# Two ones-products of the attention, moved up behind the third group of value products

## The chip, the cores and the metric

The kernel runs on one core of one Trainium2 chip. The metric is the device time of one launch in microseconds (us), as the median of several runs.

## The reference

Cut to what the change touches, the reference is a cross attention. Its queries come from `x` (2 batches, 1024 rows, width 256), its keys and values from a context of 77 rows joined to `x`, so there are 1101 keys. It has 16 heads of width 64:

```
q, k, v = split_heads(...)                       # 16 heads, 64 wide
dots = einsum('bhid,bhjd->bhij', q, k) * scale
attn = softmax(dots, axis=-1)
out  = einsum('bhij,bhjd->bhid', attn, v)
x    = x + out.reshape(...) @ Wout
```

Behind it stands a mixture of 32 experts with routing, which the change does not touch.

## The kernel before, in words

**Tiling.** Heads are worked in pairs: 8 pairs, one `turn` each. Within a pair the 2048 queries are cut into four blocks of 512 (`d` = 0 to 3; batch is `d // 2`), so the attention is 32 blocks. A block has 18 score tiles: head `h` = 0, 1 of the pair by key tile `kt` = 0 to 8 (the last has 77 keys). An event ("st", d, h, kt) is one such tile: TensorE makes scores with two products (L817, L821), ScalarE takes the exponential into `probsT` (L1458), and the event ("add", d, h, kt) adds the tile to a running row sum on GpSimd (L636).

**The other events of a block.**
- "av" (L832): two value products per key tile, accumulated in `ps_o`. Tiles 0 to 2 come at (1, 3) of the block's own walk, 3 to 5 at (1, 6), and tiles 6 to 8, the third group, only in the walk of the next block, behind its score tile (0, 5). ScalarE then copies `ps_o` to `oT` (L1446).
- "max" (L794 on TensorE, L1246 on VectorE): scores of 128 queries against all keys, reduced to the negated row maximum. The four of head 1 of a block come at (0, 0) to (0, 5) of the same block; `own_max[3]` is the last.
- "row" (L800, L1253): when the four maxima of a head are there, TensorE turns them into a row (it waits for `max_done`), and VectorE writes them into `q2`. The second score product (L821) of the head's first tile waits for that.
- "sum" (L844, L1257): two products of `rowsum` with ones give the sums over the keys for both heads. TensorE waits for the last add of that block. VectorE takes the reciprocal of the result into `rinv`.
- "norm" (L641, GpSimd): `oT` times `rinv`. "out" (L857, L1267): the product with `Wout`, added to `x_sb`.
- "k", "q", "v" (L720) project keys, queries and values for a coming block; "hi" (ScalarE, L1430, L1432) and "lo" (VectorE, L1235, L1238) split them into a high and a low part. `q_again` and `q_low`, the last parts of the query split, stand at (0, 5) in every block.

**What sets the order.** `attention_plan()` writes one list of events out by hand, and every engine walks the same list in order and does its own part of each event. Where an event stands in the list sets its place in the queue of TensorE, VectorE, ScalarE and GpSimd at once. Events in `IN_RING`, "sum" among them, take the two PSUM banks `ps_t` in turn, by their order in the list (`job_in`); an event waits until the one two places before it has released its bank.

The plan of a block is in `after`, a map from a score tile to what follows it. `prev` is the block before. In block 0 of the first pair there is no block before it, and "sum" is a placeholder that only passes its bank on; the sum of the very last block stands in the list END, behind the walk.

Of the kernel before, what the change touches and what calls it, by code (L numbers as in the profile page):

```python
# [60 lines left out]
def attention_plan():  # L61

    turn = []
    for d in range(QUADS):
        n, ahead = (d + 1) % QUADS, -int(d == LAST_D)
        prev, behind = (d - 1) % QUADS, int(d == 0)
        b = n // 2  # L70
        project = n % 2 == 0

        def nxt(*ev):
            return ev, ahead

        def own(*ev):
            return ev, 0

        def old(*ev):
            return ev, behind  # L80

        def values(make, block, kts):
            return [make("av", block, kt) for kt in kts]

        def project_q():
            return [nxt("q", b, n % 2), nxt("hi", "q", b, n % 2, (0, 1))]

        def project_k(i):
            return [nxt("k", b, i), nxt("hi", "k", b, i, (0, 1))]

        q_again, q_low = nxt("hi", "q", b, n % 2, (2, 3)), nxt("lo", "q", b, n % 2)
        k_low = [nxt("lo", "k", b, i) for i in range(3)]
        first_values = values(own, d, (0, 1, 2))
        more_values = values(own, d, (3, 4, 5))
        last_values = values(old, prev, (6, 7, 8))
        own_max = [own("max", d, 1, i) for i in range(4)]
        next_max = [nxt("max", n, 0, i) for i in range(4)]
        out = [old("out", prev, i) for i in range(2)]
        after = {(0, 8): [own("row", d, 1), old("sum", prev)],
                 (1, 1): [],  # L100
                 (1, 2): [old("norm", prev), next_max[0]],
                 (1, 3): first_values + [next_max[1]]}
        if project:
            after[0, 0] = [own_max[0]] + project_k(0) + [own_max[1], k_low[0]]
            after[0, 2] = project_k(2) + [own_max[2], k_low[2]]
            after[0, 3] = project_k(1) + [k_low[1]]
            after[0, 5] = project_q() + [q_again] + last_values + [q_low, own_max[3]]
            after[1, 4] = [out[0], next_max[2]]
            after[1, 5] = [nxt("v", b, 0), next_max[3]]
            after[1, 6] = more_values + [nxt("row", n, 0), out[1]]  # L110
            after[1, 7] = [nxt("v", b, 1)]
            after[1, 8] = [nxt("v", b, 2)]
        else:
            after[0, 0] = [own_max[0]] + project_q() + [own_max[1]]
            after[0, 3] = [own_max[2]]
            after[0, 5] = [q_again] + last_values + [q_low, own_max[3]]
            after[1, 4] = [out[0], next_max[2]]
            after[1, 6] = [out[1], next_max[3]] + more_values + [nxt("row", n, 0)]
        if d == 2:
            after[1, 1] = [(("w", 0), -1)]  # L120
        for h in range(2):
            for kt in range(KEY_TILES):
                turn += [own("st", d, h, kt)] + ([own("add", d, h, kt)] if kt else []) + after.get((h, kt), [])

    before = [("w", 0)]
    for i in (0, 2, 1):
        before += [("k", 0, i), ("hi", "k", 0, i, (0, 1)), ("lo", "k", 0, i)]
    before += [("q", 0, 0), ("hi", "q", 0, 0, (0, 1)), ("hi", "q", 0, 0, (2, 3)), ("v", 0, 0), ("max", 0, 0, 0),
               ("lo", "q", 0, 0), ("v", 0, 1), ("max", 0, 0, 1), ("v", 0, 2), ("max", 0, 0, 2), ("max", 0, 0, 3),
               ("row", 0, 0)]  # L130
    before = [(ev, -1) for ev in before]
    assert sorted(map(str, before)) == sorted(str(item) for item in turn if item[1] == -1)

    def stand_in(ev, back):
        if ev[0] == "out" and back == 1:
            return [(("cen", ev[2]), 0)]
        return [(("gap", ev), 0)] if ev[0] in IN_RING else []

    def stand_in_router(events):

        put = {("st", 2, 1, 8): [("stat", 0)],
               ("st", 3, 0, 1): [("root", 0), ("normed", 0), ("normed", 1)],
               ("st", 3, 0, 2): [("turned", 0, 0)],
               ("st", 3, 0, 3): [("low", 0, 0)],
               ("st", 3, 0, 4): [("low", 0, 1)],
               ("st", 3, 0, 5): [("low", 1, 0)],
               ("st", 3, 0, 6): [("square", 0), ("low", 1, 1)],
               ("st", 3, 0, 8): [("square", 1)]}
        done = []
        for ev, back in events:  # L150
            done += [(new, 0) for new in put.get(ev, [])]
            turned = ev[0] == "gap" and d_of(done) == LAST_D and JOB_OF_TURN.get(ev[1])
            if turned != ("turned", 0, 0):
                done.append((turned, 0) if turned else (ev, back))
        return done

    def d_of(events):
        return max((ev[1] for ev, back in events if ev[0] == "st"), default=0)

    first = [item for ev, back in turn for item in ([(ev, back)] if back < 1 else stand_in(ev, back))]  # L160
    final = [item for ev, back in turn for item in ([(ev, back)] if back >= 0 else stand_in(ev, back))]
    final = stand_in_router(final)
    end = [item for item in turn if item[1] == 1] + [(("gap", ("pad",)), 1)]
    at = [ev[0] for ev, back in end]
    end.insert(at.index("sum") + 1, (("stat", 2), 1))
    end.insert(at.index("sum") + 2, (("score", 0), 1))
    return before, first, turn, final, end


def xattn_moe(nc, x, ctx_in, ln_m_g, ln_m_b, ln_l_g, ln_l_b, Wq, Wkv, Wout, group_c, expert_c, e_bias,  # L170
# [28 lines left out]

    JOBS_A = B * DT * 2 + DT  # L200
    BEFORE, FIRST, TURN, FINAL, END = attention_plan()
    SCORES = [ev for ev, back in TURN if ev[0] == "st"]
    RING, BEFORE_RING, END_RING = ([ev[1] if ev[0] == "gap" else ev for ev, back in events
# [1403 lines left out]
```

## Time and profile before

| | |
|---|---|
| median of 3 runs | 1681.18 us (1678.7 to 1681.22) |
| span of the profiled execution, first to last instruction | 1731.2 us |
| TensorE busy in it | 1541.0 us, 89% |
| VectorE, ScalarE, GpSimd busy | 58%, 46%, 54% |
| attention blocks, from the first row product to the last block's reciprocal | 69.5 to 1122.7 us |
| mean granted TensorE clock | 0.950 of 2.4 GHz |

The page names no device time of the profiled execution other than its span. The span is 50.0 us longer than the median of the runs. In timelines each line is a run of like instructions on one engine: start, time until its end, engine, line and operation, number of instructions, and in brackets how long the engine sat idle before it and what released it. Matmul ends are modelled and reach past the start of the next matmul, so distances between starts are the better measure for TensorE. One product in full f32 shows as two MATMUL instructions.

### The profile page before, as it was taken

How to read it: one execution, taken by the hardware profiler on the slowest of the kernel's cores; microseconds unless marked ns; L12 is line 12 of the kernel's file. 1: busy time of each engine (PE TensorE's matmuls, PEld its weight loads, DVE VectorE, ACT ScalarE, POOL GpSimd, SP SyncE). 2: the span in 40 equal slices, each digit the busy share in tenths (PEclk: the TensorE clock that was granted, in tenths of full speed). 3: DMA queues.
4: the chain of work that ended last, by engine and by line, in shares of the span. 5: the costliest groups of instructions: out<-in, count | busy, mean ns of one | idle time of the engine just before them, and what ended most of it. 6: DMA issues, size and time to landing. Idle time of an engine off the chain costs nothing.

```text
span 1731.2 us, 25990 instructions
## 1 busy us (share of the span) xinstructions
PE 1541.0 (89%) x8078; PEld 1075.6 (62%) x8078; DVE 999.6 (58%) x1517; ACT 800.9 (46%) x1548; POOL 939.7 (54%) x748
## 2 busy tenths in 40 slices
PE   2799999999999999999999998853488999999995
PEld 1555555555555555555555555442477999999995
DVE  5455565565565565565565565483135666666663
ACT  2344544544544544544544544431125666666663
POOL 3366676676676676676676676535701334343433
PEclk8799999999999999999999999856798999999998
DMA  9600000000000000000000000022305667676664
GB/s 228 138 14 10 14 14 10 14 13 9 13 13 9 13 13 9 13 13 9 13 13 9 14 13 1 1 93 84 116 24 169 182 176 187 166 192 171 183 173 92
DMA packets 92700, 114.28 MB, mean 66 GB/s; under 512 B 10195, under 2 KB 71637, under 8 KB 92629
## 3 DMA queue, kind: packets, MB, share of 16 engines
q1 hardware_dynamic: 75605, 93.82, 18.8%
q0 software_dynamic: 17056, 19.97, 5.9%
q8 instruction: 20, 0.33, 0.1%
q14 instruction: 19, 0.16, 0.0%
HBM read 71.78 MB, written 35.06 MB: 62 GB/s over the span
## 4 chain that ended last, share of the span: by engine, by line
PE 80%; DVE 7%; ACT 5%; issue 3%; another core or an unknown queue 3%; DMA 1%; POOL 0%; SPq 0%; DVEq 0%; ACTq 0%; POOLq 0%
PE ps_o L832 15%; PE ps_t L720 9%; PE ps_m L794 9%; PE ps_st L817 8%; PE ps_m L720 8%; PE ps_st L720 7%; PE ps_st L821 6%; ACT arena L1458 3%; PE ps_t L857 3%; PE ps_o L913 3%; PE ps_m L913 3%; PE ps_t L844 2%; PE ps_t L939 2%; PE ps_t L800 1%
## 5 line engine op out<-in xcount | busy, mean ns | idle before, releaser
L636 POOL TENSOR_TENSOR arena<-arena 128x512 f32<-128x512 f32 (+1 forms) x512 | 656.3, 1284 | 370.9 <-ACT arena L1458 346.8
L1458 ACT ACTIVATE arena<-ps_st 128x512 f32<-128x512 f32 (+1 forms) x576 | 326.3, 595 | 434.9 <-PE ps_st L821 420.9
L1246 DVE TENSOR_REDUCE arena_r<-ps_m 128x1 fp32r<-128x1101 f32 x256 | 332.3, 1298 | 234.4 <-PE ps_m L794 230.7
L678 POOL DMA_INDIRECT acc_rows<-arena,ids x96 | 151.8, 1581 | 315.7 <-ACT arena L1555 288.2
L817 PE MATMUL ps_st<-arena_r 128*128 128x512 f32 (+1 forms) x576 | 262.6, 456 | 24.2 <-ACT arena L1458 24.2
L832 PE MATMUL ps_o<-arena 128*64 128x512 f32 (+1 forms) x1152 | 268.4, 601 | 0.0
L821 PE MATMUL ps_st<-arena_r 68*128 68x512 f32 (+2 forms) x576 | 229.6, 399 | 0.9 <-DVE arena_r L1253 0.9
L794 PE MATMUL ps_m<-arena_r 128*128 128x512 f32 (+1 forms) x768 | 193.0, 360 | 6.3 <-DVE arena_r L1246 6.3
L794 PEld LDWEIGHTS ps_m<-arena_r 128*128 128x128 f32 x768 | 134.6, 192 | 102.7 <-issue 44.6
L817 PEld LDWEIGHTS ps_st<-arena_r 128*128 128x128 f32 (+1 forms) x576 | 106.9, 186 | 111.9 <-ACT arena L1458 87.9
L1507 ACT ACTIVATE arena<-ps_m 128x320 f32<-128x320 f32 (+1 forms) x144 | 65.7, 456 | 234.6 <-PE ps_st L720 166.8
L720 PE MATMUL ps_m<-arena_r 128*128 128x320 f32 (+2 forms) x864 | 164.8, 327 | 2.1 <-DVE arena_r L1337 1.3
L832 PEld LDWEIGHTS ps_o<-arena 128*64 128x64 f32 (+1 forms) x1152 | 74.3, 136 | 141.3 <-issue 130.5
L1295 DVE TENSOR_TENSOR arena<-arena,ps_st 128x320 f32<-128x320 f32 (+1 forms) x144 | 73.2, 509 | 152.1 <-ACT arena L1507 126.2
L720 PE MATMUL ps_st<-arena_r 128*128 128x320 f32 (+2 forms) x864 | 159.1, 320 | 0.0
L1280 DVE TENSOR_TENSOR arena_r<-arena,arena_r 128x768 fp32r<-128x768 f32 x128 | 122.1, 956 | 45.4 <-ACT arena_r L1495 40.9
L720 PEld LDWEIGHTS ps_m<-arena_r 128*128 128x128 f32 x864 | 137.0, 191 | 12.0 <-issue 6.8
L720 PEld LDWEIGHTS ps_st<-arena_r 128*128 128x128 f32 x864 | 137.0, 189 | 4.3
L720 PE MATMUL ps_t<-arena_r 128*128 128x512 f32 x384 | 107.7, 418 | 10.4 <-DVE arena_r L1225 6.8
L1257 DVE RECIPROCAL arena<-ps_t 128x512 f32<-128x512 f32 x32 | 107.4, 3358 | 15.9 <-PE ps_t L844 15.9
L821 PEld LDWEIGHTS ps_st<-arena_r 68*128 68x128 f32 (+2 forms) x576 | 107.9, 187 | 11.3 <-DVE arena_r L1253 2.0
L1495 ACT ACTIVATE arena_r<-arena 128x768 fp32r<-128x768 f32 x132 | 110.3, 841 | 5.2 <-PE ps_t L913 5.2
(175 smaller groups left out, 1802.7 us busy)
## 6 DMA issues: line engine op xcount, KB each, us to landing
arena<-in_L_ffn_wg_dram SPq DMA_DIRECT2D x32, 512.0 KB
arena<-in_L_ffn_wu_dram SPq DMA_DIRECT2D x32, 512.0 KB
arena<-in_L_ffn_wd_dram SPq DMA_DIRECT2D x32, 512.0 KB
x_slots<-arena SPq DMA_DIRECT2D x5, 2176.0 KB, 19.9
arena<-x_slots SPq DMA_DIRECT2D x32, 272.0 KB, 2.7
arena_r<-arena_r SPq DMA_DIRECT2D x30, 275.2 KB, 3.6
arena<-x_slots SPq DMA_DIRECT2D x32, 68.0 KB, 2.4
x_sb<-in_x_dram SPq DMA_DIRECT2D x2, 1024.0 KB, 7.4
```

The source lines that it names most:

```text
L636: pool.tensor_tensor(acc, probsT[0:rows, h, 0, :] if kt == 1 else acc, probsT[0:rows, h, kt, :], ALU.add).then_inc(added, 1)
L678: pool.indirect_dma_start(out=dst[:, :], in_=y_sb[par][:, c, 0:w], in_offset=None, compute_op=ALU.add, out_offset=bass.IndirectOffsetOnAxi ...
L720: mm = pe.matmul(ps, a, m, start=(n == 0), stop=(n == len(pairs) - 1))
L794: mm = pe.matmul(scores_m[:, lo:lo + w], q1[h][:, c:c + P], k1[b][h][:, lo:lo + w], start=True, stop=True)
L817: pe.matmul(ps_st[0:rows, n % 2, :], k1[b][h][:, r], q1[h][:, c:c + 512], start=True, stop=False)
L821: pe.matmul(ps_st[0:rows, n % 2, :], k2[b][h][kr, r], q2[h][kr, c:c + 512], start=False, stop=True).then_inc(st_ready, 1)
L832: mm = pe.matmul(ps_o[ROWK[h], :], vals[0:rows, d // 2, kt, ROWK[h]], probsT[0:rows, h, kt, :], start=(kt == 0), stop=(kt == KT_N - 1), sk ...
L1246: dve.tensor_reduce(neg[h][:, c:c + 1], scores_m[:, 0:KEYS], AX.X, ALU.max, negate=True)\
L1257: dve.reciprocal(rinv[:, :], bank[:, :]).then_inc(free, 1)
L1280: dve.tensor_tensor(ws_lo[slot][:, c], w_raw[slot][:, c], ws_hi[slot][:, c].bitcast(F32), ALU.subtract).then_inc(w_lo_done, 1)
L1458: act.activation(probsT[0:rows, h, kt, :], ps_st[0:rows, n % 2, :], ACT.Exp)\
L1495: act.activation(ws_hi[slot][:, c], w_raw[slot][:, c], ACT.Copy).then_inc(w_hi_done, 1)
```

## The change

"sum" of the previous block leaves the place behind score tile (0, 8), where it stood behind "row", and goes to the end of `last_values`, which stands at (0, 5) in front of `q_low` and `own_max[3]`.

```diff
         more_values = values(own, d, (3, 4, 5))
-        last_values = values(old, prev, (6, 7, 8))
+        last_values = values(old, prev, (6, 7, 8)) + [old("sum", prev)]
         own_max = [own("max", d, 1, i) for i in range(4)]
...
-        after = {(0, 8): [own("row", d, 1), old("sum", prev)],
+        after = {(0, 8): [own("row", d, 1)],
                  (1, 1): [],
```

The two uses of `last_values`, unchanged by the diff:

```
after[0, 5] = project_q() + [q_again] + last_values + [q_low, own_max[3]]   # d = 1, 3
after[0, 5] = [q_again] + last_values + [q_low, own_max[3]]                 # d = 0, 2
```

## Rows read from the trace of the kernel before

**Rows 1.** The page: span, busy time of TensorE, engine shares of the chain

```profile
span 1731.2 us, 25990 instructions
...
PE 1541.0 (89%) x8078; PEld 1075.6 (62%) x8078; DVE 999.6 (58%) x1517; ACT 800.9 (46%) x1548; POOL 939.7 (54%) x748
...
PE 80%; DVE 7%; ACT 5%; issue 3%; another core or an unknown queue 3%; DMA 1%; POOL 0%; SPq 0%; DVEq 0%; ACTq 0%; POOLq 0%
```

**Rows 2.** Busy time by stretch, attention: start:end, length, busy per engine, clock, DMA

```profile
89.70:1076.00 986.30, 962.59 (x4307) 567.89 (x4306) 590.62 (x555) 460.16 (x837) 658.17 (x516) 1.00 0.05 12
```

**Rows 3.** The waits of TensorE's matmuls: us in total, times, longest

```profile
PE ps_st L817 <- ACT arena L1458: 24.2, 95, 1.6
...
PE ps_m L794 <- DVE arena_r L1246: 6.3, 6, 3.1
...
PE ps_st L821 <- DVE arena_r L1253: 0.9, 2, 0.5
```

**Rows 4.** Timeline of TensorE, a block with d = 1

```profile
504.65 0.78 PE L794 MATMUL ps_m<-arena_r 128*128 128x512 f32 x3
...
507.24 0.49 PE L800 MATMUL ps_t<-ident,arena_r 128*128 128x512 f32 x1
507.67 1.08 PE L844 MATMUL ps_t<-arena,ones 128*64 128x512 f32 x4
508.68 0.51 PE L817 MATMUL ps_st<-arena_r 128*128 128x512 f32 x1
...
511.81 2.79 PE L832 MATMUL ps_o<-arena 128*64 128x512 f32 x12
```

**Rows 5.** Timeline of VectorE: the reciprocal of the block before, then the same block

```profile
476.36 3.36 DVE L1257 RECIPROCAL arena<-ps_t 128x512 f32<-128x512 f32 x1 [0.34 <-PE ps_t L844]
...
504.46 1.39 DVE L1238 SCALAR_TENSOR_TENSOR arena_r<-ps_t,arena_r 64x512 fp32r<-64x512 f32 x2 [2.16 <-ACT arena_r L1432]
505.88 1.30 DVE L1246 TENSOR_REDUCE arena_r<-ps_m 128x1 fp32r<-128x1101 f32 x1
...
508.79 3.36 DVE L1257 RECIPROCAL arena<-ps_t 128x512 f32<-128x512 f32 x1 [0.34 <-PE ps_t L844]
512.07 1.24 DVE L1246 TENSOR_REDUCE arena_r<-ps_m 128x1 fp32r<-128x1101 f32 x1
```

**Rows 6.** The instructions of L1257: shortest, median, longest ns, first and last start

```profile
L1257 DVE RECIPROCAL arena<-ps_t x32: 3357/3358/3358, 119.1 to 1119.3; 128x512 f32<-128x512 f32 x32
```

**Rows 7.** Timeline of TensorE, the block with d = 2 that follows

```profile
537.29 0.77 PE L794 MATMUL ps_m<-arena_r 128*128 128x512 f32 x3
...
539.82 0.39 PE L800 MATMUL ps_t<-ident,arena_r 128*128 128x512 f32 x1
540.14 1.08 PE L844 MATMUL ps_t<-arena,ones 128*64 128x512 f32 x4
```

**Rows 8.** Timeline of GpSimd: last add of the block before that one

```profile
528.38 1.30 POOL L636 TENSOR_TENSOR arena<-arena 77x512 f32<-77x512 f32 x1 [0.99 <-ACT arena L1458]
```

**Rows 9.** Timeline of TensorE, the very first block, which has no sum

```profile
84.44 0.47 PE L800 MATMUL ps_t<-ident,arena_r 128*128 128x512 f32 x1 [1.54 <-DVE arena_r L1246]
...
85.69 0.79 PE L821 MATMUL ps_st<-arena_r 128*128 128x512 f32 x1 [0.54 <-DVE arena_r L1253]
...
89.74 2.80 PE L832 MATMUL ps_o<-arena 128*64 128x512 f32 x12
```

**Rows 10.** Busy time by stretch, around that first block's row; the clock is third from the end

```profile
85.00:86.00 1.00, 0.46 (x2) 0.31 (x2) 0.63 (x1) 0.00 (x0) 0.89 (x1) 0.84 0.00 0
...
88.00:89.00 1.00, 1.00 (x3) 0.75 (x3) 0.00 (x0) 0.57 (x1) 1.00 (x1) 0.50 0.00 0
89.00:90.00 1.00, 1.00 (x6) 0.53 (x6) 0.69 (x1) 0.17 (x2) 1.00 (x2) 0.95 0.00 0
```

**Rows 11.** The same view earlier, a longer low stretch: its first and last slice of 1 us

```profile
69.00:70.00 1.00, 0.46 (x1) 0.49 (x2) 0.39 (x1) 0.00 (x0) 0.00 (x0) 0.50 0.94 200
...
75.00:76.00 1.00, 1.00 (x6) 0.81 (x5) 0.00 (x0) 0.46 (x1) 0.00 (x0) 0.78 0.00 0
```

## The prediction

> **What bounds the kernel now.** I read the page first: TensorE is busy most of the span and carries 80% of the chain that ended last [rows 1]. An average hides stages, so I then took the stretch of the attention: from 89.70 to 1076.00 TensorE is busy for 962.6 of 986.3 us at a granted clock of 1.00, that is 2.4 GHz [rows 2]. Only 23.7 us of it are idle. Then the list of waits: in the whole span TensorE's matmuls of the attention wait 24.2 us for exponentials, 6.3 us for a maximum and 0.9 us for a row [rows 3]. So nearly nothing is left to win here by shifting work, and whatever makes TensorE wait is paid in full. Last I read one block's timeline on TensorE beside the same on VectorE, because VectorE must do something between any two steps that the change swaps [rows 4, 5, 7].
>
> **What is moved.** Each engine walks one list, so the move is made in every queue. On TensorE the two ones-products (four instructions, 508.68 - 507.67 = 1.01 us from start to start [rows 4]) go ahead of `own_max[3]`, three score tiles and "row". No product is added, so their work costs nothing by itself. On VectorE the reciprocal goes ahead of `q_low`, the reduction of `own_max[3]` and "row". It is 3.36 us long in all 32 cases [rows 6]. ScalarE, GpSimd and SP issue nothing for "sum". "norm" on GpSimd keeps its place at (1, 2) and finds `rinv` ready earlier, which wins at most a part of the 23.7 us of rows 2, since "out" on TensorE is what waits for it. No DMA moves.
>
> **Can the sum run that early?** It waits for the last add of the block before, which ends at 528.38 + 1.30 = 529.68 [rows 8]; the sum would start at 537.29, where the third value products are through [rows 7]. That is 7.6 us of slack, so this wait costs nothing. The banks: "sum" and "row" change places in the ring. "sum" then takes the bank of the last `k` or `v` product before it, released well before; "row" takes that of `q`, released by `q_low`, which VectorE does anyway before the maximum that "row" waits for. Nothing is added.
>
> **Where the path breaks.** "row" on TensorE waits for `max_done` of `own_max[3]`. Now that reduction is short of work ahead of it: `q_low` starts at 504.46, the reduction at 505.88, and it ends at 507.18; "row" starts at 507.24, just as the last score tile is through [rows 4, 5]. So the wait is already on the edge, and any delay on VectorE there shows on TensorE. From the start of the sum in its new place:
> - VectorE: 1.12 us until the reciprocal starts (508.79 - 507.67), 3.28 until the next instruction (512.07 - 508.79), 1.42 for the two halves of `q_low` (505.88 - 504.46), 1.30 for the reduction, 0.06 until "row" starts [rows 4, 5]. Sum 7.18 us.
> - TensorE: 1.01 for the sum, then `own_max[3]` and three score tiles, 507.24 - 504.65 = 2.59 us in blocks with d = 1, 3 [rows 4] and 539.82 - 537.29 = 2.53 us in the others [rows 7]. Sum 3.60 and 3.54 us.
>
> TensorE waits for the difference, 3.58 and 3.64 us, mean **3.61 us a block**. Behind the waiting "row" stand the first score tile of head 1 and so all of ScalarE's exponentials and GpSimd's adds. They can't help.
>
> **What follows the row.** Until now the sum stood between "row" and the first score tile and gave VectorE 1.01 us in which to write `q2`. That cover is gone: the second score product waits for it. The trace has this case: in the very first block "sum" is only a placeholder. There "row" came 1.54 us late, the second score product then waited 0.54 us, and from "row" to the first value product it took 89.74 - 84.44 = 5.30 us [rows 9]. In a normal block it is 511.81 - 507.24 = 4.57 us, less 1.01 for the sum, 3.56 [rows 4]. The difference is **1.74 us**: 0.54 of wait, and 1.20 because the granted clock fell to 0.50 (1.2 GHz). It fell in the slice from 85 to 86, whose mean is 0.84, and was back early in the slice from 89 to 90, whose mean is 0.95 [rows 10]. If TensorE loses the clock after a wait of 1.54 us, I expect it after one of 3.61 us. For the cost of that I have bounds: nothing, if the clock stays, and 3.2 us, if it stays low as long as in the longer low stretch (below). I take 1.20, since that row is nearest in place and in what follows.
>
> The Trainium skill, TensorE: Matmul & The Clock Gate, section Terms, gives the penalty as throttled time times (1 - K/N), half the throttled time here. In the first block that would be half of about 3.4 us (85.68 to 89.10 from the two slice means), 1.7 us in place of 1.20; the trace gives less, since TensorE was waiting for part of it. By the page's figure the sum below would be 31 x 5.86 = 182 us and the time 1863 us.
>
> **The sum.** 3.61 + 0.54 + 1.20 = 5.35 us a block. The move counts in 31 of the 32 blocks: the first has no sum, and the sum of the last stands in the end list, which the change leaves in its order. 31 x 5.35 = 165.9 us. The profiled execution would have a span of 1731.2 + 165.9 = 1897 us. The page gives no other time for it, and its span is 50.0 us (3%) above the median of the runs; I add the same microseconds to the median: 1681.2 + 165.9 = **1847 us**. If everything in the timed runs is 3% shorter, it is 161 us and 1842.
>
> **Rivals.**
> - *The clock stays at 2.4 GHz.* Then only the waits count: 31 x 4.15 = 129 us, **1810 us**. For it: the blocks are otherwise dense, with 0.24 us idle per 10 us [rows 2]. Against it: the first block [rows 9, 10]. Chance 0.20.
> - *The clock stays low for longer.* Near 70 us it was low from before 69.00 to about 75.44 (slice mean 0.78), some 6.4 us [rows 11]. Half of that is 3.2 us a block: 31 x (3.61 + 0.54 + 3.2) = 228 us, **1909 us**. Against it: TensorE was waiting several times in that stretch, which a block here does once. Chance 0.13.
> - *Something takes up most of the wait*, so that a block loses less than 3.8 us and the time stays under 1800 us: for instance the exponential waits of 24.2 us [rows 3] go away, and TensorE reaches "row" later for another cause. What TensorE waits for now is too little for that. Chance 0.03.
> - *The other side: the reciprocal was in the way where it stood.* Now the next maximum is reduced at 512.07, the moment the reciprocal is through [rows 5]. Freed of it, VectorE could run ahead for the next block, and TensorE would lose its present waits, at most the 23.7 us idle of rows 2: **1657 us**. It decides only if VectorE gets from the new sum to the end of the maximum in about 3.6 us; it needs 7.18, of which the reciprocal alone is 3.28. And TensorE shows nearly no wait for a maximum to win [rows 3]. Chance 0.03 (0.02 faster, 0.01 no change).
> - That the change does nothing is excluded by the list: it is one list for all engines, and both places are reached in 31 blocks.
>
> **The numbers.** The forecast has 0.61. Its own range is 1823 (all present idle time of rows 2 gone) to 1863. The range for 8 in 10 takes in the clock that stays and part of the way to the longer low stretch: 1800 to 1895 us. Some 0.2%, 3.4 us, is what a measurement of this kernel can tell from no change. Faster 0.02, same 0.01, slower 0.97.
>
> **What would show it.** In the changed profile: the reciprocal starts 1.1 us after the sum, right behind the third value products; `q_low` starts at its end with no idle time of its own; "row" (L800) has some 3.6 us of idle time before it, released by the maximum (L1246), in 31 blocks, near 112 us in total; L821 waits for L1253 in each block, near 17 us in total; the mean granted clock of the attention falls below 1.00, with a low stretch in each block. The distance between two reciprocals grows from 508.79 - 476.36 = 32.4 us [rows 5] to near 37.8. The expert stage is as before. I am wrong if "row" has no wait, if VectorE does `q_low` before the reciprocal, or if the clock stays at 1.00, which would give the first rival.

## The result, and the profile after

The changed kernel takes **1866.11 us** (median of 4 runs, 1858.18 to 1866.26) against 1680.62 us before (4 runs, 1678.7 to 1681.22). The ratio is 1.109, interval 1.107 to 1.111: 185.5 us slower, 6.0 us for each of the 31 blocks that the move reaches. The forecast was 1847 us, range 1800 to 1895.

One caution on the spans. That of the profile before (1731.2 us) has a disturbance of some 50 us behind the attention: from the end of its last reciprocal to the end it takes 608.5 us, in the changed kernel 1856.4 - 1302.8 = 553.6 us. So differences are taken between run times, or within the attention.

The page of the changed kernel, to be read against [rows 1]:

```profile
span 1856.4 us, 25990 instructions
...
PE 1601.1 (86%) x8078; PEld 1107.4 (60%) x8078; DVE 1005.5 (54%) x1517; ACT 804.2 (43%) x1548; POOL 938.4 (51%) x748
...
PE 76%; DVE 13%; issue 6%; ACT 3%; DMA 1%; POOL 0%; DVEq 0%; SPq 0%; ACTq 0%; POOLq 0%
```

The number of instructions is the same. VectorE's share of the chain (the work that ended last, followed back from the end) went from 7% to 13%, though VectorE is busy for only 6 us more than before. TensorE is busy for 60 us more with the same products, which fits its lower granted clock: 0.91 on average from 113 to 1250 us, against 1.00 in the attention before [rows 2]. The list of waits of TensorE's matmuls names the first cause, to be read against [rows 3]:

```profile
PE ps_t L800 <- DVE arena_r L1246: 108.3, 32, 3.6
...
PE ps_st L817 <- ACT arena L1458: 16.0, 64, 0.8
PE ps_st L821 <- DVE arena_r L1253: 13.2, 33, 0.5
```

"row" (L800) waits 3.6 us at the longest for the maximum; before it was 3.0 us in all. The wait of L821 for VectorE's write of the row is new as well, 0.9 us before. Waits for exponentials fell by 8 us. The place where they went is the one behind the row: at 510.10 TensorE waited 0.22 us for an exponential, and at 585.75 in the changed kernel, where it runs at the lower clock, it doesn't wait. That ScalarE catches up during the long wait is not the reason: with the same pause and the clock at full speed (E9 below) the list has 23.5 us again.

The timeline of TensorE in a block with d = 1, against [rows 4]:

```profile
572.83 2.80 PE L832 MATMUL ps_o<-arena 128*64 128x512 f32 x12
575.46 1.03 PE L844 MATMUL ps_t<-arena,ones 128*64 128x512 f32 x4
576.42 0.78 PE L794 MATMUL ps_m<-arena_r 128*128 128x512 f32 x3
...
582.71 0.80 PE L800 MATMUL ps_t<-ident,arena_r 128*128 128x512 f32 x1 [3.60 <-DVE arena_r L1246]
583.30 0.63 PE L817 MATMUL ps_st<-arena_r 128*128 128x512 f32 x1
584.27 0.80 PE L821 MATMUL ps_st<-arena_r 128*128 128x512 f32 x1 [0.35 <-DVE arena_r L1253]
...
585.75 0.80 PE L817 MATMUL ps_st<-arena_r 128*128 128x512 f32 x1
...
588.82 2.79 PE L832 MATMUL ps_o<-arena 128*64 128x512 f32 x12
```

And VectorE beside it, against [rows 5]:

```profile
576.54 3.36 DVE L1257 RECIPROCAL arena<-ps_t 128x512 f32<-128x512 f32 x1 [3.33 <-PE ps_t L844]
579.93 1.39 DVE L1238 SCALAR_TENSOR_TENSOR arena_r<-ps_t,arena_r 64x512 fp32r<-64x512 f32 x2
581.35 1.30 DVE L1246 TENSOR_REDUCE arena_r<-ps_m 128x1 fp32r<-128x1101 f32 x1
583.54 0.68 DVE L1253 TENSOR_TENSOR arena_r<-ps_t,mask 4x512 fp32r<-4x512 f32 x1 [0.89 <-PE ps_t L800]
```

VectorE goes from the reciprocal to `q_low` to the maximum without idle time: 582.71 - 575.46 = 7.25 us from the sum to "row", of which TensorE can fill 3.6. Before the reciprocal it stood idle for 3.33 us. In the kernel before, `q_low` started 504.46 - 501.92 = 2.54 us after the value products; counted from 572.83 that is 575.37, 1.2 us ahead of the reciprocal, so most of `q_low` would have fitted in front of it. The start of the value products in the kernel before, in front of [rows 4]:

```profile
501.92 2.80 PE L832 MATMUL ps_o<-arena 128*64 128x512 f32 x12
```

The clock by slices of 1 us around the same row (third figure from the end), against [rows 10]:

```profile
544.00:545.00 1.00, 0.46 (x3) 0.12 (x1) 0.68 (x1) 0.00 (x0) 0.00 (x0) 0.69 0.00 0
551.00:552.00 1.00, 1.00 (x6) 0.29 (x4) 0.00 (x0) 0.00 (x0) 1.00 (x2) 0.90 0.00 0
581.00:582.00 1.00, 0.00 (x0) 0.00 (x0) 0.97 (x2) 0.00 (x0) 0.92 (x2) 0.96 0.00 0
582.00:583.00 1.00, 0.29 (x1) 0.29 (x2) 0.65 (x1) 0.00 (x0) 0.47 (x1) 0.50 0.00 0
588.00:589.00 1.00, 1.00 (x4) 0.35 (x5) 1.00 (x1) 0.07 (x1) 1.00 (x1) 0.62 0.00 0
589.00:590.00 1.00, 1.00 (x6) 0.30 (x6) 0.24 (x1) 0.52 (x1) 1.00 (x2) 1.00 0.00 0
```

The granted clock falls to 0.50 (1.2 GHz) at 581.9, while TensorE still waits, and is back at 588.8 (0.62 is 0.24 us at full clock): 6.8 us low. In the block before, whose row starts at 543.62, it fell at 544.4 (0.69 in that slice) and was back at 551.2: 6.8 us as well. The same view over the whole attention has a low stretch at each of the 30 rows that waited 3.4 us or more: 6.8 us long at 24 of them, 10.2 at four, 3.4 at two. In the very first block of the kernel before it had been 3.4 us. From row to value products it takes 588.82 - 582.71 = 6.11 us, where the first block took 5.30.

### The profile page after: what moved, and what is told of

Same layout as the page of the kernel before. It is cut to its first block, busy times and chain, and to the rows that moved or that the text cites. A ratio compares the mean times of both kernels' runs of the same rounds, so it can differ in the third digit from the quotient of the medians.

```text
span 1856.4 us, 25990 instructions
## 1 busy us (share of the span) xinstructions
PE 1601.1 (86%) x8078; PEld 1107.4 (60%) x8078; DVE 1005.5 (54%) x1517; ACT 804.2 (43%) x1548; POOL 938.4 (51%) x748
## 3 DMA queue, kind: packets, MB, share of 16 engines
q1 hardware_dynamic: 75605, 93.82, 17.5%
## 4 chain that ended last, share of the span: by engine, by line
PE 76%; DVE 13%; issue 6%; ACT 3%; DMA 1%; POOL 0%; DVEq 0%; SPq 0%; ACTq 0%; POOLq 0%
PE ps_o L832 14%; PE ps_t L720 9%; PE ps_m L720 8%; PE ps_m L794 8%; PE ps_st L720 7%; PE ps_st L817 7%; PE ps_st L821 7%; DVE arena_r L1246 3%; PE ps_t L857 3%; PE ps_o L913 2%; PE ps_m L913 2%; DVE arena_r L1238 2%; PE ps_t L800 2%; PE ps_t L939 2%; PE ps_t L844 2%
## 5 line engine op out<-in xcount | busy, mean ns | idle before, releaser
L636 POOL TENSOR_TENSOR arena<-arena 128x512 f32<-128x512 f32 (+1 forms) x512 | 655.0, 1279 | 553.6 <-ACT arena L1458 530.1
L817 PE MATMUL ps_st<-arena_r 128*128 128x512 f32 (+1 forms) x576 | 286.3, 497 | 16.0 <-ACT arena L1458 16.0
L832 PE MATMUL ps_o<-arena 128*64 128x512 f32 (+1 forms) x1152 | 276.2, 615 | 0.0
L821 PE MATMUL ps_st<-arena_r 68*128 68x512 f32 (+2 forms) x576 | 260.3, 452 | 13.2 <-DVE arena_r L1253 13.2
L794 PEld LDWEIGHTS ps_m<-arena_r 128*128 128x128 f32 x768 | 146.8, 208 | 107.3 <-issue 50.3
L794 PE MATMUL ps_m<-arena_r 128*128 128x512 f32 (+1 forms) x768 | 204.7, 378 | 6.3 <-DVE arena_r L1246 6.2
L817 PEld LDWEIGHTS ps_st<-arena_r 128*128 128x128 f32 (+1 forms) x576 | 120.6, 209 | 81.7 <-ACT arena L1458 59.6
L1257 DVE RECIPROCAL arena<-ps_t 128x512 f32<-128x512 f32 x32 | 107.4, 3358 | 107.1 <-PE ps_t L844 107.1
L821 PEld LDWEIGHTS ps_st<-arena_r 68*128 68x128 f32 (+2 forms) x576 | 122.2, 212 | 45.1 <-DVE arena_r L1253 34.3
L720 PEld LDWEIGHTS ps_m<-arena_r 128*128 128x128 f32 x864 | 136.1, 190 | 10.8 <-issue 6.7
L800 PE MATMUL ps_t<-ident,arena_r 128*128 128x512 f32 x64 | 38.8, 607 | 110.3 <-DVE arena_r L1246 108.3
```

Of the source, the lines that this page charges most:

```text
L636: pool.tensor_tensor(acc, probsT[0:rows, h, 0, :] if kt == 1 else acc, probsT[0:rows, h, kt, :], ALU.add).then_inc(added, 1)
L720: mm = pe.matmul(ps, a, m, start=(n == 0), stop=(n == len(pairs) - 1))
L794: mm = pe.matmul(scores_m[:, lo:lo + w], q1[h][:, c:c + P], k1[b][h][:, lo:lo + w], start=True, stop=True)
L800: pe.matmul(bank[:, :], neg[h], ident4[:, :, :].rearrange("p a n -> p (a n)"), start=True, stop=True).then_inc(job_ready[jn % 2], 1)
L817: pe.matmul(ps_st[0:rows, n % 2, :], k1[b][h][:, r], q1[h][:, c:c + 512], start=True, stop=False)
L821: pe.matmul(ps_st[0:rows, n % 2, :], k2[b][h][kr, r], q2[h][kr, c:c + 512], start=False, stop=True).then_inc(st_ready, 1)
```

## The experiments

The theory: VectorE's one queue now has the reciprocal ahead of the last maximum and of `q_low`; TensorE waits for that, and the waits cost it the clock. The rival: the cost lies on TensorE's side, in the order of its products or in the changed turn of the two `ps_t` banks. Two further questions: how much is the clock, and was the reciprocal in the way at its old place?

**E1, the reciprocal alone at its old place.** The ones-products stay at (0, 5) as in the changed kernel; VectorE takes the reciprocal at a new event behind "row".

```diff
-        after = {(0, 8): [own("row", d, 1)],
+        after = {(0, 8): [own("row", d, 1), old("recip", prev)],
...
-                    if kind == "sum":
+                    if kind == "recip":
+                        jn, more = own_job(("sum", a), turn)
+                        bank, free = ps_t[jn % 2], job_free[jn % 2]
```

> The products with ones stand at their new place, VectorE's reciprocal at its old one. My theory (the reciprocal queued ahead of the last maximum makes TensorE wait at the row): L800 has no wait for the maximum worth naming; only the cover behind the row is gone, so L821 waits about 0.5 us a block for L1253, 31 x 0.5 = 17 us, and the time is about 1697 us; somewhat more if those short waits cost TensorE's clock. Rival (the cost lies in TensorE's own order or in the changed turn of the two ps_t banks): near the changed kernel, 1866 us.

Measured: **1692.02 us**, ratio 1.007 (1.005 to 1.009). Its waits:

```profile
PE ps_st L817 <- ACT arena L1460: 24.0, 95, 0.9
...
PE ps_st L821 <- DVE arena_r L1253: 17.5, 33, 0.5
...
PE ps_m L794 <- DVE arena_r L1246: 6.7, 6, 3.1
```

The wait of "row" for a maximum stands further down with 3.0 us in all, as before; the 17.5 us of L821 are the lost cover. So TensorE's order and the banks, both as in the changed kernel, cost 11 us of the 185. The rival falls. It is 5 us cheaper than expected. A part of that can be read from starts: behind the value products, TensorE goes on to the sum after 575.46 - 572.83 = 2.63 us, where it took 504.65 - 501.92 = 2.73 to go on to `own_max[3]` before, and the sum itself takes 576.42 - 575.46 = 0.96 in place of 1.01 [rows 4]. E1 has the same 2.63 and 0.96. That is 0.15 us a block, 4.7 us in all.

**E2, `q_low` ahead of the sum.**

```diff
-            after[0, 5] = [q_again] + last_values + [q_low, own_max[3]]
+            after[0, 5] = [q_again] + last_values + [q_low] + ones_sum + [own_max[3]]
```

(The same in the line for d = 1, 3, with `last_values` without the sum and `ones_sum = [old("sum", prev)]`.)

> As the changed kernel, but q_low stands ahead of the sum, so the reciprocal no longer delays it. My theory: the path on VectorE from the sum to the row is 7.18 - 1.42 = 5.76 us, against 3.57 on TensorE, so L800 waits 2.2 us a block (about 68 us in all, 108.3 in the changed kernel), L821 0.4 us as there. If the clock falls as in the changed kernel (about 2.3 us a block), the time is 1680.6 + 31 x 4.9 = 1833 us; if it costs only the 1.2 us that the first block shows, 1799 us. Rival (TensorE's order or the banks): 1866 us, since they are unchanged.

Measured: **1834.22 us**, ratio 1.092 (1.090 to 1.093).

```profile
PE ps_t L801 <- DVE arena_r L1247: 66.9, 32, 2.3
...
PE ps_st L818 <- ACT arena L1459: 15.9, 64, 0.8
...
PE ps_st L822 <- DVE arena_r L1254: 12.3, 33, 0.5
```

The wait of the row (one line lower here) is 66.9 us for an expected 68, longest 2.3. Taking 1.4 us of other work out of VectorE's path takes 1.3 us off each wait. The price of the clock stayed: the waits shrank by 41 us, the time by only 32, and the low stretches at the rows are 6.8 us long as in the changed kernel.

**E3, idle products in the wait, in the row's bank.** Ahead of the row's wait for the maximum:

```diff
+                        for _ in range(14 * h):
+                            pe.matmul(bank[:, :], ident4[:, 0, :], ident4[:, :, :].rearrange("p a n -> p (a n)"),
+                                      start=True, stop=True)
                         pe.wait_ge(max_done, hp * MAX_HP + d * 8 + h * 4 + 4 + 1)
```

> The changed kernel with 14 idle products (identity by identity, into the row's own bank, overwritten by the row) ahead of each wait of a head-1 row, some 0.235 us each, 3.3 us a block, so that TensorE works where it waited. My theory (what the changed kernel loses beyond its waits is the granted clock): clock of the attention back at 1.00, the waits themselves stay as filled or idle time, 31 x (3.6 + 0.5) = 127 us, time about 1808 us. Rival (the rest is lost elsewhere, not in the clock): 1866 us or above. If 14 products outlast the wait, a few us more.

Measured: **1895.08 us**, ratio 1.129 (1.127 to 1.131). The experiment was badly built: the row's bank is now that of `q`, released by `q_low`, so the fill itself had to wait and came behind it, as the timeline of TensorE shows:

```profile
592.26 5.07 PE L800 MATMUL ps_t<-ident 128*128 128x512 f32 x14 [2.26 <-DVE arena_r L1241]
597.17 0.39 PE L803 MATMUL ps_t<-ident,arena_r 128*128 128x512 f32 x1
```

The fill made the block longer instead of filling the wait. The mean clock over the span rose to 0.954, but since the fill came on top of a wait, its cost can't be parted from the clock's. The run does show the bank wait that I had passed over as harmless: harmless for "row", not for anything put before it. The 5.07 us of the 14 products also mislead, because a low stretch of 3.4 us lies over them. A block earlier the same 14 ran at full clock, in 557.14 - 553.81 = 3.33 us, 0.24 each:

```profile
553.81 3.49 PE L800 MATMUL ps_t<-ident 128*128 128x512 f32 x14 [2.08 <-DVE arena_r L1241]
557.14 0.40 PE L803 MATMUL ps_t<-ident,arena_r 128*128 128x512 f32 x1
```

The clock in the two fills (third figure from the end):

```profile
555.00:556.00 1.00, 1.00 (x7) 0.79 (x5) 0.09 (x1) 0.00 (x0) 0.12 (x1) 1.00 0.00 0
...
594.00:595.00 1.00, 1.00 (x4) 0.71 (x4) 0.00 (x0) 0.00 (x0) 0.00 (x0) 0.50 0.00 0
```

**E4, a copy in place of the reciprocal**, in the changed kernel. It leaves out the division by the sums:

```diff
-                        dve.reciprocal(rinv[:, :], bank[:, :]).then_inc(free, 1)
+                        dve.tensor_copy(rinv[:, :], bank[:, :]).then_inc(free, 1)
```

> The changed kernel with a plain copy in place of the reciprocal, so the division by the sums is left out (rinv holds the sums). About 0.69 us in place of 3.36. My theory: the path on VectorE is 7.18 - 2.67 = 4.5 us against 3.57, so L800 waits some 0.9 us a block and L821 0.5: 31 x 1.4 = 45 us, time about 1725 us if the clock holds, up to 1760 if it falls in part of the blocks. Rival (TensorE's order or the banks): 1866 us, since only the length of one VectorE instruction changes.

Measured: **1760.8 us** (1746.53 to 1783.42), ratio 1.044 (1.039 to 1.049) without the longest run. The copy takes 0.69 us, and the row's wait is down to 29.2 us, of which 3.0 stood there before: 0.85 us a block.

```profile
PE ps_t L800 <- DVE arena_r L1246: 29.2, 32, 1.5
```

With TensorE's program untouched, the length of one VectorE instruction decides 105 us. The clock is lost in part of the blocks even with so short a wait: 21 of 30 rows of the attention have a low stretch at them, 9 have none. The runs spread over 37 us where other kernels' spread over 8.1 or less, and their order is that of their mean clock: 1746.5 us at 0.948, 1760.7 and 1761.0 at 0.937, 1783.4 at 0.924. That is one and the same kernel, paying more or less for the clock.

**E5, 9 idle products that wait for nothing late.** Behind score tile (0, 8), into the `ps_st` bank that the next score tile overwrites:

```diff
+                    if kind == "row" and ev[2] == 1:
+                        at = SCORES.index(("st", a, 1, 0))
+                        pe.wait_ge(exp_done, hp * ST_HP + at + 1)
+                        for _ in range(9):
+                            pe.matmul(ps_st[:, at % 2, :], ident4[:, 0, :], ident4[:, :, :].rearrange("p a n -> p (a n)"),
+                                      start=True, stop=True)
```

> The changed kernel with 9 idle products (identity by identity) behind score tile (0, 8), now into the bank of ps_st that the next score tile overwrites, so that they need not wait for the row's bank, which q_low releases. The earlier fill took 5.07 us for 14 products, 0.36 each, so 9 are 3.2 us of the 3.6 us wait. If what the changed kernel loses beyond its waits is the granted clock: clock of the attention near 1.00, L800 waits some 0.4 us a block, time 1680.8 + 31 x (3.5 + 0.4) = 1802 us, 60 us below the changed kernel though TensorE has more to do. Rival (the rest is not the clock): 1866 us or more.

Measured: **1836.12 us**, ratio 1.093 (1.092 to 1.095), 30 us below the changed kernel. The products were shorter than reckoned, 0.25 us each, since the 0.36 came from the fill of E3 at the lower clock. So 1.3 us of wait were left in the block shown:

```profile
607.04 2.27 PE L761 MATMUL ps_st<-ident 128*128 128x512 f32 x9
610.61 0.50 PE L806 MATMUL ps_t<-ident,arena_r 128*128 128x512 f32 x1 [1.29 <-DVE arena_r L1252]
```

Half of the expected gain. The direction was right, the amount open, so the fill was made longer.

**E9, the same with 14.**

> As the fill of 9 products, with 14. In that run the 9 took 2.27 us from start to start, 1.3 us of wait were left ahead of the row, and the mean clock of the attention rose from 0.91 to 0.96. 14 products are 3.5 us and leave next to no wait. If the loss beyond the waits is the clock: clock near 1.00 in the attention, time 1680 + 31 x (3.6 + 0.5) = 1807 us, below the fill of 9 (1836 us) with more work done. Rival (the loss has another cause): as the fill of 9 or above, 1836 us or more.

Measured: **1806.07 us**, ratio 1.075 (1.073 to 1.077), for an expected 1807. The fill covers the wait:

```profile
630.05 3.42 PE L761 MATMUL ps_st<-ident 128*128 128x512 f32 x14
633.80 0.50 PE L806 MATMUL ps_t<-ident,arena_r 128*128 128x512 f32 x1 [0.33 <-DVE arena_r L1252]
```

And the clock of the attention is back, in the busy time by stretch:

```profile
120.00:1050.00 930.00, 891.15 (x3969) 541.46 (x3969) 500.74 (x462) 385.10 (x700) 554.74 (x433) 1.00 0.04 10
```

TensorE does 14 more products a block and the kernel is 60 us faster than the changed one. This takes the loss apart: **126 us are waits** (1806 - 1680), 4.06 us a block, and **60 us are the clock** (1866 - 1806), 1.9 us a block. The 60 us are a net figure: the changed kernel has 12 us less of the short waits than E9 (L817 16.0 against 23.5 us, L821 13.2 against 17.6), which its slower TensorE hides.

The mean clock over the whole span says the same, in order the changed kernel and E9:

```profile
core 0: 1856.4 us, clock 0.915
```

```profile
core 0: 1803.9 us, clock 0.970
```

At two levels, the share at the lower one is twice what is missing to 1: 2 x 0.085 x 1856 = 316 us and 2 x 0.030 x 1804 = 108 us. So 208 us more at 1.2 GHz cost 1858.2 - 1805.7 = 52 us in these two executions, a quarter and not the half. Part of the reason can be read in the block shown: of the 6.8 us, TensorE was idle for 0.8 ahead of "row" (582.71 - 581.92) and 0.35 behind it, and the wait for an exponential that it has at full clock was not there.

**E6, the sum behind `own_max[3]`.**

```diff
-            after[0, 5] = [q_again] + last_values + [q_low, own_max[3]]
+            after[0, 5] = [q_again] + last_values + [q_low, own_max[3]] + ones_sum
```

> The sum at (0, 5), but behind own_max[3]. My theory (an order on VectorE): the maximum is no longer late, so L800 has no wait; but the reciprocal now stands ahead of VectorE's part of the row: it starts near 507.2 in the times of the kernel before, ends at 510.5, the row is written by 511.2 and L821, due at 508.9, waits 2.3 us a block for L1253, 31 x 2.35 = 73 us in all. With a clock loss of 1.4 to 2.8 us a block as in the copy and q_low runs: 1797 to 1840 us. Rival (only the delay of the maximum matters): about 1692 us, as with the late reciprocal.

Measured: **1794.45 us**, ratio 1.069 (1.067 to 1.072), just below the expected span of 1797 to 1840. The wait moved to where the theory put it:

```profile
PE ps_st L822 <- DVE arena_r L1254: 63.0, 33, 2.3
```

VectorE has the reciprocal ahead of the row's write: it starts at 551.22 and the write follows at 554.60 without idle time.

```profile
551.22 3.35 DVE L1258 RECIPROCAL arena<-ps_t 128x512 f32<-128x512 f32 x1
554.60 0.68 DVE L1254 TENSOR_TENSOR arena_r<-ps_t,mask 4x512 fp32r<-4x512 f32 x1
```

So the delay of the maximum isn't the point by itself. The two short urgent steps of VectorE, the maximum and the row's write, both pay when the reciprocal is ahead of them.

**E7, the same copy in the kernel before**, without the division here too.

> The kernel before with a copy in place of the reciprocal: the division by the sums is left out. If the reciprocal at its old place is fully hidden (my theory), only the last one, behind the last block, is on the path: 2.7 us less, 1678 us. Rival (the other side: the reciprocal was in the way where it stood): TensorE's waits in the attention shrink, 1657 to 1670 us.

Measured: **1678.28 us**, ratio 0.999 (0.998 to 1.000), expected 1678. An instruction that is 2.67 us shorter in every block gains 1.7 us in all. At its old place it was hidden.

**E8, the two ones-products taken apart**, head 0 behind tile (0, 7), as a new event `half`, and head 1 at the old place, in the kernel before:

```diff
+                 (0, 7): half_sum,
...
-                        for h in range(2):
-                            mm = pe.matmul(bank[ROWK[h], :], ones[:, 0:DH], rowsum[:, a % 2, h, :],
-                                           start=True, stop=True, skip_group_check=True)
+                        mm = pe.matmul(bank[ROWK[1], :], ones[:, 0:DH], rowsum[:, a % 2, 1, :],
+                                       start=True, stop=True, skip_group_check=True)
```

> The kernel before with its two products with ones taken apart: head 0 behind score tile (0, 7), head 1 where both stood, behind the row. If the waits for exponentials ahead of tile (0, 8), some 0.22 us a block, can be covered with 0.5 us of other work while 0.5 us behind the row still covers VectorE's write: 31 x 0.22 = 7 us less, 1674 us. Rival (the wait only moves to the next tile, or VectorE's write shows): 1681 us or a few more.

Measured: **1697.42 us**, ratio 1.010 (1.009 to 1.012), a miss. The waits for exponentials fell as expected, from 24.2 to 15.8 us. But one product alone costs as much as the pair did: 514.36 - 513.36 = 1.00 us, against 1.01 for both [rows 4]. With 0.38 us won by each wait that is gone (start to start, see E10), 31 x (1.00 - 0.38) = 19 us more were due; 17 are measured.

```profile
513.36 1.07 PE L852 MATMUL ps_t<-arena,ones 128*64 128x512 f32 x2
514.36 0.45 PE L819 MATMUL ps_st<-arena_r 128*77 128x512 f32 x1
```

**E10 and E11, moves into small waits** of the kernel before. E10 puts `next_max[0]` one tile earlier; E11 also moves the next block's "row" from (1, 6) to (1, 7) for d = 0, 2.

```diff
-                 (1, 1): [],
-                 (1, 2): [old("norm", prev), next_max[0]],
+                 (1, 1): [next_max[0]],
+                 (1, 2): [old("norm", prev)],
...
-            after[1, 1] = [(("w", 0), -1)]
+            after[1, 1] = [(("w", 0), -1), next_max[0]]
```

> The kernel before with next_max[0] moved from behind tile (1, 2) to behind tile (1, 1). Its products, 0.5 us on TensorE, then stand where TensorE waits 0.22 us for an exponential, and VectorE is at the reciprocal until later anyway. My theory (this kernel's small waits can be covered by work moved into them, if no queue gets a longer path): L817's waits fall from 24 to some 17 us, time 31 x 0.22 = 7 us less, 1673 us. Rival (the wait only moves on to tile (1, 3)): 1680 us.

> As the run with next_max[0] moved up, and in blocks with d = 0, 2 the row of the next block goes from (1, 6) to (1, 7), which puts 0.33 us of TensorE's work ahead of the wait at the next block's first tile. Further 16 x 0.22 = 3.5 us less than that run, 1670 us, if VectorE still writes the row in time (0.54 + 0.68 us from the row's start, L821 comes about 1.1 us after it). Rival: L821 now waits some 0.1 to 0.5 us in these blocks, and nothing is won or up to 8 us lost.

Measured: E10 **1665.27 us**, ratio 0.991 (0.990 to 0.993); E11 **1662.14 us**, ratio 0.990 (0.988 to 0.991). Both are about 1% faster than the kernel before. E11's median is 3.1 us below E10's, for an expected 3.5, but their runs overlap (E10 1663.8 to 1666.8, E11 1661.6 to 1665.1), so the further step is likely and not shown. The waits for exponentials in E10:

```profile
PE ps_st L817 <- ACT arena L1458: 17.0, 65, 1.6
```

They fell by 7 us as expected, but the time fell by 15. A wait costs more than the list shows: with its end modelled long, a matmul hides part of the gap behind it. The timeline of the kernel before shows it at the place in question:

```profile
509.02 0.39 PE L821 MATMUL ps_st<-arena_r 128*128 128x512 f32 x1
509.25 0.39 PE L817 MATMUL ps_st<-arena_r 128*128 128x512 f32 x1
509.49 0.40 PE L821 MATMUL ps_st<-arena_r 128*128 128x512 f32 x1
510.10 0.50 PE L817 MATMUL ps_st<-arena_r 128*128 128x512 f32 x1 [0.22 <-ACT arena L1458]
```

From start to start, L821 to the next L817 takes 0.23 us without a wait and 0.61 with one that is listed as 0.22. That is 0.38 us, 31 x 0.38 = 12 us, most of the 15; the rest is open.

## Why the prediction was right, and what was mis-sized

The sum came out 19 us low (1847 for 1866 us), inside the range of 1800 to 1895 and 3 us outside the own range of the forecast, 1823 to 1863.

- **What bounds the kernel** held: the attention was dense on TensorE, and E7 shows that nothing was to be won from the reciprocal at its old place. The rival on the other side, 1657 us, falls with it (1678).
- **The sum can run that early**: right. The changed kernel's list has a single wait of L844 for an add, 0.4 us, and the kernel before has it too.
- **Where the path breaks**: right in place and size. 3.61 us a block were forecast ahead of "row", 112 us in all; 108.3 us are listed, 3.0 of them there before, and single rows wait 3.6 us (d = 1, 3) and 3.4 us (d = 0, 2) where 3.58 and 3.64 were forecast. E1, E2 and E4 change one term of that path each and move the wait as its sum says (about none, 2.1 and 0.9 us a block).
- **The banks, "nothing is added"**: E1 agrees for the change as made. E3 shows that the swap did move the point from which the row's bank is free; the prediction should have named this.
- **The lost cover behind the row**: forecast 0.54 us a block, listed as 13.2 us in all, 17.5 where the clock stays (E1). With the row's wait it was to be 4.15 us a block; E9 gives 4.06, and its 1806 us the first rival's 1810.
- **The clock: the term that was mis-sized.** I took 1.20 us a block from the first block, on the ground that it was nearest in place and in what follows. It measured 1.9 (E9 against the changed kernel). The step that failed is taking the row of a 1.54 us wait for one of 3.6 us: the low stretch is 6.8 us at 24 of 30 rows, where it was 3.4. In its length it is the stretch of the second rival (near 70 us, chance 0.13), so that rival had the mechanism and not the price: 3.2 us took half of the stretch, and a low microsecond cost a quarter. The forecast had the price of a low microsecond about right (1.20 us for 3.4) and half of the length. That 1847 is so near is in part luck: the first block's short stretch came with a higher price per microsecond than the long ones have. With 1.9 in place of 1.20 the sum is 1680.6 + 31 x (4.15 + 1.9) = 1868 us; measured 1866.
- By the rule of the Trainium skill (TensorE: Matmul & The Clock Gate, section Terms) a throttled stretch costs half its time, and the prediction got 1863 us from it. This case's traces don't bear the half out: 52 us for 208 us (E9) are a quarter. 1863 is close by two errors that offset each other, since the stretch was also twice as long as put in.
- **Of the signs to look for**, the distance of two reciprocals was to be 37.8 us; it is 38.7 in one pair (615.27 - 576.54). L821 was to wait near 17 us in total; 13.2 are listed, less because of the lower clock, as E9's 17.6 shows.

Not settled: why the low stretch is 3.4 us after one wait and 6.8 or more after another, and how short a wait may be to keep the clock. E4 lost it in part of its blocks at 0.85 us a block; E1, with 0.5 us behind the row, lost it in none.

## What to carry to other kernels

When one list orders all engines, cost a move on every queue that it changes: here TensorE's share of the event was harmless (E1, 11 us), and VectorE's 3.36 us instruction, put ahead of two short urgent ones, cost the rest. Compare the two paths to the next meeting point from the common start, 7.2 us against 3.6; only their difference is paid, and then the clock on top, for which the row to go by is one with a wait as long as the one expected. A fill of idle work in the wait, in a buffer that is free early, is a clean way to part the clock from the wait; and the gain in such a dense kernel was in the small repeated waits, which cost more than they are listed with.

## What the runs showed of the hardware

- TensorE runs two f32 products with 64 columns each, one into the lower and one into the upper half of the bank's partitions, in the time of one: 1.01 us for the pair, 1.00 us for one alone (E8). Parting such a pair doubles its cost.
- How much low clock the waits bring, as the sum over slices of 1 us from 113 us to the last block's reciprocal or its copy (twice what is missing to 1):

| kernel | wait of the row a block | time at 1.2 GHz |
|---|---|---|
| before | none | 14 us |
| E9 | 0.3 us | 14 us |
| E4 | 0.85 us | 120 us |
| E5 | 1.4 us | 96 us |
| E6 (wait behind the row) | 2.0 us | 141 us |
| E2 | 2.1 us | 218 us |
| changed | 3.5 us | 222 us |

  Cutting the wait from 3.5 to 2.1 us won nothing of the clock, and 0.85 us still cost more of it than 1.4 us did with nine products ahead of them. So the length of the wait alone doesn't order these runs.
- One idle product of 512 columns takes 0.24 us from start to start at a granted clock of 1.00 (E3, 14 in 3.33 us). Where the clock was 0.50 for 3.4 us of it, the same 14 took 4.91 us.
